# A routed two-choice network block: the residual written to the output early, and the experts' rows added to it in memory

## The chip, the cores and the metric

The kernel runs on one core of one Trainium2 chip. A core has five engines that run side by side: TensorE (PE in the profile; the loading of its weights is PEld), VectorE (DVE), ScalarE (ACT), GpSimd (POOL) and SyncE (SP), which here does nothing but issue transfers. The transfers themselves run on 16 DMA engines of the core, whoever issues them. The metric is the time of one execution on the device in microseconds (us).

## What is computed

Two layers work on `x`, 16 sequences of 128 tokens of 128 numbers. Each adds a block to the residual; only the end of the second matters here:

```python
x = x + _L0_ffn_ref(_L0_cond_ref(x, ...), ...)      # attention, then a dense network
x = x + _L1_ffn_ref(_L1_cond_ref(x, ...), ...)      # attention, then 8 experts, two choices per token
...
logits = x @ gate_w.T + gate_b                       # in _L1_ffn_ref, E, K = 8, 2; CAP = 320
probs = jax.nn.softmax(logits, axis=-1)
topk_prob, topk_idx = jax.lax.top_k(probs, K)
for c in range(K):
    buf_idx = jnp.where(pos < CAP, idx * CAP + pos, n_slots)
    xbuf = jnp.zeros((n_slots, Dm), x.dtype).at[buf_idx].set(x, mode='drop')
    hmid = jax.nn.relu(jnp.einsum('ecd,edf->ecf', xb, W1) + b1[:, None, :])
    yb = jnp.einsum('ecf,efd->ecd', hmid, W2) + b2[:, None, :]
    y = y + ytok * (prb * keep.astype(prb.dtype))[:, None]
```

So each of the 2048 tokens gets, on top of the residual, one row of 128 numbers from the expert of its first choice and one from that of its second.

## The kernel before

The residual stays in SBUF as `X` (128 tokens of each sequence on the partitions, 16 sequences, 128 numbers). The program goes through attention of the first layer (one batch per sequence), its dense network (four groups of four sequences), attention of the second layer (16 batches again, with the routing of earlier batches between them), and then the eight experts. Everything is float32. Each engine has its own written order; semaphores join them.

**Routing.** When a group of tokens is routed, POOL sends each row of `Y` (the normed token, its number and its weights) by an indirect DMA to the slot that its choice gives it, in one of two buffers in device memory, `slot_rows0` and `slot_rows1` (`scatter`, L637). Empty slots hold a row with a token number of 2048 and above.

**An expert** (`expert` on PE, DVE and ACT) works on 640 slots, 320 of each choice, in five tiles of 128 rows: SP loads them into `xb` (L482), PE turns them (L1122), multiplies by W1 (L1132), DVE and ACT add the bias and cut at zero (L1926, L1361), PE multiplies by W2 (L1142), DVE adds the second bias into `yb` (L1934), ACT scales by the token's weight (L1368). `yb` lies in `hT` for even experts and in `qn` for odd ones.

**The sends.** POOL sends the finished rows back, six indirect DMAs per expert, 48 in all, first and second choice in turn:

```python
SENDS = [(0, 0, P, 0), (2, DH, P, 1), (1, 0, P, 0), (3, 0, P, 1), (2, 0, DH, 0), (4, 0, P, 1)]   # tile, rows from, to, choice
```

The row's number says where it goes, in `choice_rows0` or `choice_rows1` (`back_d`), two buffers in device memory that were cleared in the first layer (`clear_back`, L468) and have 128 rows more than there are tokens, for the empty slots. Before a send, POOL waits until the tile is ready (`e_y`) and until the send before of the same choice has landed (`e_sent0`, `e_sent1`). DVE overwrites an expert's token numbers (`tags`, L1948) only when the sends of two experts before have landed.

**The end.** When all sends have landed, SP loads both buffers into `wide_buf` (L534, eight loads), DVE adds them to `X` (L1960, eight adds), SP stores `X` to the output (L538, four stores).

**SP in the second layer.** For each batch SP waits for the values `vp` and spreads them in six small transfers (L489, L492); behind them, in batches 2 to 7, it loads the weights of one expert (L474, L475).

Of the kernel before, what the change touches and what calls it, by code (L numbers as in the profile page):

```python
# [22 lines left out]
F32 = mybir.dt.float32  # L23
# [4 lines left out]
ALU = mybir.AluOpType  # L28
# [3 lines left out]
P = 128  # L32
NB = 16
# [4 lines left out]
EXPERTS = 8  # L38
CAP = 320
TOPK = 2  # L40
# [3 lines left out]
TOKENS = NB * P  # L44
BACK = TOKENS + P
# [15 lines left out]
LATE_DMAS = 6  # L61
REL_ROW = 6 * QB
REL_USED = 5 * QB
SCRATCH_ALL = 2 + 16 * (TOPK + TOPK * NB // 4)
FAR = -1e30
MASKED = -1e20
LN_EPS = 1e-5
# [2 lines left out]
def build(nc, a, out):  # L70
    ctx = ExitStack()
    with ctx:
        def sb(name, shape, dt=F32):
            return ctx.enter_context(nc.sbuf_tensor(name, shape, dt))
# [4 lines left out]
        def sem(name):  # L79
            return ctx.enter_context(nc.semaphore(name))  # L80

        def dram(name, shape, dt=F32):
            return nc.dram_tensor(name, shape, dt).ap()

        def at(ap, offset, dims):
            return bass.AP(ap.tensor, offset, dims)
# [1 line left out]

        rel_d = dram("rel_scratch", ((HEADS - 1) * QB * (REL_ROW - 1) + QB * REL_ROW,))
        slot_d = [dram(f"slot_rows{c}", (SLOTS + P, ROW)) for c in range(TOPK)]  # L90
        back_d = [dram(f"choice_rows{c}", (BACK, P)) for c in range(TOPK)]


        X = sb("X", [P, NB, P])
# [121 lines left out]
        wide_buf = sb("wide_buf", [P, TOPK * NB * P])  # L216
        empty = sb("empty", [P, ROW])
        zero_row = sb("zero_row", [P, 4, P])
# [12 lines left out]
              for v in (hT[:].rearrange("p i d -> p (i d)"), qn[:])]  # L231

        masked_bias = [wide_buf[:, i * BIAS_AT[-1]:(i + 1) * BIAS_AT[-1]] for i in range(2)]
        back = wide_buf[:].rearrange("p (c t d) -> p c t d", c=TOPK, t=NB)


        WoT = qsq[:].rearrange("p h d -> p (h d)")[:, 0:8 * P].rearrange("p (j d) -> p j d", j=8)
# [50 lines left out]
        s = {n: sem(n) for n in names}  # L288
# [12 lines left out]
        for n in ["ln_var", "ln_rstd", "g_T_psum", "g_rows", "g_WoT", "g_psum", "g_ready", "r_le", "r_exp",  # L301
                  "r_oh", "r_pos_read", "r_pos_psum", "r_pay", "slots_out0", "slots_out1",
                  "e_w", "e_x0", "e_x1",
                  "e_T_psum", "e_T", "e_h_psum", "e_h_act", "e_h_dve", "e_y_psum", "e_y_add", "e_y",
                  "back_in0", "back_in1", "back_in2", "back_in3", "z_step", "final_out",
                  "e_sent0", "e_sent1", "e_tags"]:
            s[n] = sem(n)

# [3 lines left out]
        def unit_bias(layer, u):  # L312
            return bias[layer][:, BIAS_AT[u]:BIAS_AT[u + 1]].rearrange(
                "p (h e k) -> p h e k", h=2, e=2)
# [13 lines left out]
        def over(eng, count, body, first=2, last=2):  # L328

            for t in range(first):  # L330
                body(t, t % 2)
            with eng.Fori(first // 2, (count - last) // 2) as k:
                body(2 * k, 0)
                body(2 * k + 1, 1)
            for t in range(count - last, count):
                body(t, t % 2)
# [20 lines left out]
        def no(t, value):  # L357
            return isinstance(t, int) and t == value
# [3 lines left out]
        def _(sp):  # L362
# [72 lines left out]
            for u in range(UNITS):  # L435
                v = unit_bias(0, u).rearrange("p h e k -> p (h e) k")
# [5 lines left out]
            def later_weights():  # L442
                spread(g_out[0][:], "L0_cond_g_out", P, late_in)
                sp.dma_start(Wq[1][:], a["L1_cond_Wq"]).then_inc(attw_in, 16)
                sp.dma_start(Wkv[1][:], a["L1_cond_Wkv"]).then_inc(attw_in, 16)
                sp.dma_start(Wo[1][:, :, 0:P], a["L1_cond_Wo"].rearrange("(j p) d -> p j d", p=P)).then_inc(attw_in, 16)
                for e in range(2):
                    sp.dma_start(Wkk[:, e, :], a["L1_cond_Wkv"][:, 0:DH]).then_inc(attw_in, 16)
                spread(fb2[:], "L0_ffn_b2", P, late_in)
                spread(g_out[1][:], "L1_cond_g_out", P, late_in)  # L450
                spread(gate_b[:], "L1_ffn_gate_b", EXPERTS, late_in)
                spread(mb2[:].rearrange("p e d -> p (e d)"), "L1_ffn_b2", EXPERTS * P, late_in)
                sp.dma_start(gate_rows[:], a["L1_ffn_gate_w"]).then_inc(late_in, 16)
# [11 lines left out]
                sp.dma_start(at(slot_d[c], 0, [[ROW, P], [P * ROW, SLOTS // P], [1, ROW]]),  # L465
                             empty[:].unsqueeze(1).broadcast_to([P, SLOTS // P, ROW])).then_inc(scratch_out, 16)

            def clear_back(c):  # L468
                for r in range(0, NB, 4):
                    sp.dma_start(at(back_d[c], r * P * P, [[P, P], [P * P, 4], [1, P]]),  # L470
                                 zero_row[:]).then_inc(scratch_out, 16)

            def load_expert(e):
                sp.dma_start(eW[e][:, 0, :], a["L1_ffn_W1"][e]).then_inc(s["e_w"], 16)  # L474
                sp.dma_start(eW[e][:, 1, :].rearrange("p (j d) -> p j d", j=FB),  # L475
                             a["L1_ffn_W2"][e].rearrange("(j p) d -> p j d", p=P)).then_inc(s["e_w"], 16)
# [7 lines left out]
            def spread_values(layer):  # L484
                def batch(b, i):
                    B = b + NB * layer
                    sp.wait_ge(s["v_ready"], B + 1)
                    for g in range(4):
                        sp.dma_start(vp_u0[i][QB * g:QB * (g + 1), g // 2, DH * (g % 2):DH * (g % 2 + 1)],  # L489
                                     vp[i][0:QB, :]).then_inc(s[f"vp_in{i}"], 16)  # L490
                    for e in range(2):
                        sp.dma_start(vp_u1[i][DH * e:DH * (e + 1), DH * e:DH * (e + 1)],  # L492
                                     vp[i][0:DH, :]).then_inc(s[f"vp_in{i}"], 16)
                    if layer == 0 and no(b, 0):
                        later_weights()
                    if layer == 0 and isinstance(b, int) and 1 <= b <= UNITS:
                        second_table(b - 1)
                    if layer == 0 and isinstance(b, int) and b in (5, 6):
                        clear_slots(b - 5)
                    if layer == 0 and isinstance(b, int) and b in (7, 8):  # L500
                        clear_back(b - 7)
                    if layer == 0 and isinstance(b, int) and b in (9, 10):
                        load_expert(b - 9)

                    if layer == 1 and no(b, 2):
                        sp.wait_ge(s["f_o_psum"], NB)
                    if layer == 1 and isinstance(b, int) and 2 <= b < EXPERTS:
                        load_expert(b)

                over(sp, NB, batch, EXPERTS if layer else 12)  # L510
# [15 lines left out]
                    sp.wait_ge(s["e_tags"], e + 1)  # L526
                    load_slots(e + 2, i)

            for c in range(TOPK):
                sp.wait_ge(s[f"e_sent{c}"], 16 * 3 * EXPERTS)  # L530
            for q in range(4):
                for c in range(TOPK):
                    src = at(back_d[c], 4 * q * P * P, [[P, P], [P * P, 4], [1, P]])
                    sp.dma_start(back[:, c, 4 * q:4 * q + 4, :], src).then_inc(s[f"back_in{q}"], 16)  # L534
            out_v = out.rearrange("b n d -> n b d")
            for q in range(4):
                sp.wait_ge(s["z_step"], 2 * (q + 1))
                sp.dma_start(out_v[:, 4 * q:4 * q + 4, :], X[:, 4 * q:4 * q + 4, :]).then_inc(  # L538
                    s["final_out"], 16)
            sp.wait_ge(s["final_out"], 64)  # L540


        @block.gpsimd
        def _(pool):
# [92 lines left out]
            def scatter(t, g):  # L637
                if t == GROUPS[0][0]:
                    pool.wait_ge(scratch_out, SCRATCH_ALL)
                if t == GROUPS[g][0]:  # L640
# [64 lines left out]
            for g in range(QUADS):  # L705
                v = X[:, 4 * g:4 * g + 4, :]
# [36 lines left out]
            def send(e, i):  # L743
                for n, (t, p0, p1, c) in enumerate(SENDS):
                    sent = 16 * 3 * e + 16 * (n // 2)
                    apart(pool, (s["e_y"], TILES * e + t + 1), (s[f"e_sent{c}"], sent))
                    pool.indirect_dma_start(back_d[c], bass.IndirectOffsetOnAxis(  # L747
                        tags[i][0:p1 - p0, t if p0 == 0 else TILES, 0:1].bitcast(U32), 0), yb[i][p0:p1, t, :],
                                            None).then_inc(s[f"e_sent{c}"], 16)

            over(pool, EXPERTS, send)


        @block.tensor
# [632 lines left out]
        def _(dve):  # L1387
# [565 lines left out]

            over(dve, EXPERTS, expert)
            result(EXPERTS - 1, 1, 1)
            for q in range(4):
                dve.wait_ge(s[f"back_in{q}"], 16 * TOPK)
                for c in range(TOPK):
                    v = X[:, 4 * q:4 * q + 4, :]
                    dve.tensor_tensor(v, v, back[:, c, 4 * q:4 * q + 4, :], ALU.add).then_inc(s["z_step"], 1)  # L1960
                    dve.wait_ge(s["z_step"], 2 * q + c + 1)


INPUTS = ["x", "cond_64", "fside_16xSxS_0", "mask_BxS_bf1", "mask_BxS_bk0", "L0_cond_g_norm", "L0_cond_Wq",
# [24 lines left out]
```

## Time and profile before

| | |
|---|---|
| time, median of 3 runs | 630.7 us (625.11 to 631.92) |
| the profiled execution | 627.16 us |
| its span in the profile | 625.4 us, so 1.8 us lie around the span |
| busy PE, DVE, ACT, POOL | 496.7, 433.3, 378.6, 309.3 us |
| mean granted TensorE clock | 0.933 of full speed |
| moved by DMA | 30.02 MB |

The span begins with the first instruction and ends with the last event. Busy times are sums of an engine's instructions; engines overlap. Times in rows are counted from the start of the span. An entry such as `[0.60 <-issue]` is the time that the engine stood idle before the instruction, and what ended it; "issue" means that the profile names nothing.

### The profile page before, as it was taken

To read this page: it belongs to the slowest core of one execution; us is meant where nothing else is said; L and a number is where in the kernel's file an instruction comes from. 1 tells how busy PE (TensorE), PEld (TensorE's weight loads), DVE (VectorE), ACT (ScalarE), POOL (GpSimd) and SP (SyncE) were. 2 spreads that over 40 slices of the span, in tenths; PEclk is the share of its full clock that TensorE was granted. 3 is DMA by queue.
4 is the path that set the end of the run, shared out by engine and by line. 5 is a ranking of instruction groups with operands and counts; after the bars stand their busy time and mean duration, and the time that the engine had idled before them with its cause. 6 is when DMAs were issued, how large, how long until landed. Compare 5 with 4: busy or idle time off the path is not lost.

```text
span 625.4 us, 13829 instructions
## 1 busy us (share of the span) xinstructions
PE 496.7 (79%) x3220; PEld 399.7 (64%) x3220; DVE 433.3 (69%) x2147; ACT 378.6 (61%) x1474; POOL 309.3 (49%) x366
## 2 busy tenths in 40 slices
PE   1366999999999978895799989988987707999940
PEld 0145777767777766564688878877875605887830
DVE  4496899999999986373668888889888631434323
ACT  1156788888888865671588878777866202444420
POOL 4282756656565641755433433533664460555560
PEclk9988899999999989996899999999999767999995
DMA  4640003723100000000011121000011112222117
GB/s 133 164 135 11 13 23 74 134 74 106 38 6 6 6 7 1 0 2 2 8 40 40 50 63 39 7 4 7 25 27 38 32 46 57 64 77 59 56 38 205
DMA packets 53302, 30.02 MB, mean 48 GB/s; under 512 B 19533, under 2 KB 49670, under 8 KB 53254
## 3 DMA queue, kind: packets, MB, share of 16 engines
q1 hardware_dynamic: 50694, 24.57, 15.6%
q0 software_dynamic: 2560, 4.90, 2.4%
q8 instruction: 18, 0.29, 0.2%
q14 instruction: 30, 0.25, 0.1%
HBM read 16.13 MB, written 11.22 MB: 44 GB/s over the span
## 4 chain that ended last, share of the span: by engine, by line
PE 46%; DVE 22%; issue 15%; SPq 4%; ACT 4%; POOL 3%; DMA 3%; DVEq 1%; ACTq 0%; POOLq 0%
PE psS L850 8%; DVE sc L1540 6%; PE psS L1142 5%; PE psQ L823 4%; PE psA L905 4%; PE psO L886 3%; PE psQ L1132 3%; PE psQ L807 3%; DVE centred L1601 2%; DVE OT L1561 2%; PE psT L868 2%; PE psO L1132 1%; PE psA L1132 1%; PE psQ L1066 1%; DVE qn L1531 1%
## 5 line engine op out<-in xcount | busy, mean ns | idle before, releaser
L1228 ACT ACTIVATE sc<-sc,negmax 128x97 f32<-128x97 f32 (+3 forms) x512 | 178.9, 353 | 36.8 <-DVE negmax L1540 35.5
L850 PE MATMUL psS<-kk,qT 128*128 128x194 f32 (+3 forms) x512 | 106.0, 330 | 29.1 <-DVE negmax L1540 27.2
L850 PEld LDWEIGHTS psS<-kk,qT 128*128 128x128 f32 x512 | 79.7, 195 | 56.0 <-issue 52.6
L1540 DVE CUSTOM_DVE_ANT_0 sc<-psS,wide_buf 128x97 f32<-128x97 f32 (+3 forms) x512 | 93.2, 237 | 29.9 <-PE psS L850 26.6
L632 POOL TENSOR_TENSOR wide_buf<-bias,mask 128x132 f32<-128x132 f32 (+3 forms) x128 | 108.8, 875 | 4.2 <-DVE negmax L1540 4.2
L1228 ACT ACTIVATION_READ_ACCUMULATOR sc<-sc,negmax 128x1 f32 x512 | 97.1, 190 | 0.0
L580 POOL TENSOR_TENSOR qrn<-qssc,half 128x9 f32<-128x9 f32 (+1 forms) x32 | 55.9, 1748 | 68.3 <-DVE qssc L1526 68.2
L1552 DVE TENSOR_TENSOR pn<-sc,rsum 128x128 f32<-128x128 f32 (+3 forms) x128 | 72.5, 566 | 8.0 <-DVE rsum L1548 0.2
L905 PE MATMUL psA<-Wo,OT 128*128 128x128 f32 (+1 forms) x512 | 66.0, 284 | 1.7 <-DVE OT L1561 1.7
L905 PEld LDWEIGHTS psA<-Wo,OT 128*128 128x128 f32 x512 | 63.0, 197 | 2.7 <-DVE OT L1561 2.5
L1561 DVE TENSOR_SCALAR OT<-psO,cols 128x512 f32<-128x512 f32 x64 | 47.6, 744 | 3.2 <-PE psO L886 1.8
L1241 ACT COPY PT<-psT 96x512 f32<-96x512 f32 x64 | 37.0, 577 | 14.5 <-PE psT L868 13.6
L868 PE MATMUL psT<-ident,pn 128*96 128x128 f32 (+1 forms) x256 | 40.2, 280 | 4.3 <-issue 2.2
L1540 DVE DVE_READ_ACCUMULATOR2_ANT negmax<- 128x1 f32 x512 | 41.3, 81 | 0.5 <-issue 0.5
L886 PE MATMUL psO<-PT,vp 96*64 96x256 f32 (+1 forms) x256 | 34.8, 390 | 7.3 <-DVE OT L1561 4.5
L644 POOL DMA_INDIRECT slot_rows<-Y,dest_u x32 | 31.3, 979 | 17.5 <-issue 7.2
L868 PEld LDWEIGHTS psT<-ident,pn 128*96 128x96 f32 (+1 forms) x256 | 28.6, 138 | 16.9 <-issue 16.3
L747 POOL DMA_INDIRECT choice_rows<-hT,tags x24 | 22.5, 939 | 32.7 <-ACT hT L1368 20.7
L807 PE MATMUL psQ<-Wq,xnT 128*128 128x512 f32 x64 | 36.6, 658 | 0.9 <-ACT qT L1210 0.2
L1210 ACT ACTIVATE qT<-psQ 128x512 f32<-128x512 f32 x64 | 34.6, 587 | 2.9 <-PE psQ L836 2.5
L615 POOL TENSOR_TENSOR vp<-kvs,vnull 128x64 f32<-128x64 f32 x32 | 11.7, 365 | 47.1 <-PE psO L886 47.0
L823 PE MATMUL psQ<-xnT,Wq 128*128 128x128 f32 x256 | 33.5, 287 | 0.0
(297 smaller groups left out, 1006.5 us busy)
## 6 DMA issues: line engine op xcount, KB each, us to landing
slot_rows<-empty SPq DMA_DIRECT2D x2, 1390.0 KB, 9.8
xb<-slot_rows SPq DMA_DIRECT2D x16, 139.0 KB
vp_u<-vp SPq DMA_DIRECT2D x128, 8.0 KB, 1.8
choice_rows<-zero_row SPq DMA_DIRECT2D x8, 256.0 KB, 3.0
wide_buf<-choice_rows SPq DMA_DIRECT2D x8, 256.0 KB, 4.7
Wq<-in_L_cond_Wq SPq DMA_DIRECT2D x2, 512.0 KB, 5.0
vp_u<-vp SPq DMA_DIRECT2D x64, 16.0 KB, 1.8
eW<-in_L_ffn_W SPq DMA_DIRECT2D x4, 256.0 KB, 2.9
```

Source lines behind the costliest of these rows:

```text
L580: pool.tensor_tensor(dst, src, half[:, 0:k], ALU.pow).then_inc(done, count)
L632: pool.tensor_tensor(unit_masked(i, u).rearrange("p h e k -> p (h e) k"), unit_bias(layer, u).rearrange("p h e k -> p (h e) k"), mask[laye ...
L807: pe.matmul(psQ[:, h, :], xnT[i][:], Wq[0][:, 512 * h:512 * (h + 1)], start=True, stop=True).then_inc(s["q_psum"], 1)
L823: m = pe.matmul(psQ[:, h, j * P:(j + 1) * P], Wq[1][:, (4 * h + j) * P:(4 * h + j + 1) * P], xnT[i][:], start=True, stop=True)
L850: m = pe.matmul(psS[:, h, 0:2 * w], qT[i][:, h, u].rearrange("p m q -> p (m q)"), kk[i][:, :, 0:w], start=True, stop=True)
L868: m = pe.transpose(psT[0:k, probs_bank(u, i), g * P:(g + 1) * P], pn[u][:, g, :], ident[:])
L886: m = pe.matmul(psO[DH * e:DH * (e + 1), 2 * P * (u - 2):2 * P * (u - 1)], vp[i][0:k, :], PT[u - 1][0:k, :, e, :], start=True, stop=True)
L905: m = pe.matmul(psA[:, Y_AT[layer]:4 * P], OT[i][:, j].rearrange("p u q -> p (u q)"), Wo[layer][:, j, :], start=(j == 0), stop=(j == 7))
L1228: m = act.activation(v, v, ACT.Exp, bias=negmax[:, u, g:g + 1], scale=-1.0, accum_out=psum_row[:, u, g:g + 1])
L1540: dve.tensor_tensor_reduce(sc[u][:, h, e, :], unit_psum(u)[:, h, e, :], unit_masked(i, u)[:, h, e, :], -1.0, -FAR, ALU.add, ALU.min, accum ...
L1552: dve.tensor_tensor(pn[u][:], sc[u][:].rearrange("p h e k -> p (h e) k")[:, :, 1:k + 1], rsum[:, u, :].unsqueeze(2).broadcast_to([P, 4, k] ...
L1561: dve.tensor_scalar(OT[i][:, :, 2 * half_of:2 * half_of + 2, :], psO[:].rearrange("p (u j q) -> p j u q", u=2, q=QB), cols[:, C_VN:C_VN + ...
```

## The change

- The residual is stored to the output by SP behind the spreads of batch 4 of the second layer (`store_residual`): four stores of 256 KB and one of zeros. The output has 128 rows more, which the caller drops; empty slots go there.
- First-choice sends go to the output itself and add to what is there (`compute_op=ALU.add`). Second-choice sends go, as before, plainly, to a cleared buffer, now `second_rows`. One clearing of the first layer falls away.
- POOL waits for the five stores before the first send. Behind the last send it waits for all sends and issues one transfer that adds the 2048 rows of `second_rows` to the output, from device memory to device memory, as 128 pieces of 8 KB.
- The eight loads, the eight adds of DVE and the four stores at the end fall away. SP ends by waiting for this last transfer.

```diff
-        back_d = [dram(f"choice_rows{c}", (BACK, P)) for c in range(TOPK)]
+        second_d = dram("second_rows", (BACK, P))
+        sums_d = out.rearrange("b n d -> (b n) d")
+        back_d = [sums_d, second_d]
...
+            def store_residual():
+                for q in range(4):
+                    sp.dma_start(out[4 * q:4 * q + 4].rearrange("b n d -> n b d"),
+                                 X[:, 4 * q:4 * q + 4, :]).then_inc(s["final_out"], 16)
+                sp.dma_start(sums_d[TOKENS:BACK, :], zero_row[:, 0, :]).then_inc(s["final_out"], 16)
...
-                    if layer == 0 and isinstance(b, int) and b in (7, 8):
-                        clear_back(b - 7)
+                    if layer == 0 and no(b, 7):
+                        clear_second()
+                    if layer == 1 and no(b, 4):
+                        sp.wait_ge(s["f_x"], NB)
+                        store_residual()
...
-            for c in range(TOPK):
-                sp.wait_ge(s[f"e_sent{c}"], 16 * 3 * EXPERTS)
-            for q in range(4):
-                for c in range(TOPK):
-                    src = at(back_d[c], 4 * q * P * P, [[P, P], [P * P, 4], [1, P]])
-                    sp.dma_start(back[:, c, 4 * q:4 * q + 4, :], src).then_inc(s[f"back_in{q}"], 16)
-            out_v = out.rearrange("b n d -> n b d")
-            for q in range(4):
-                sp.wait_ge(s["z_step"], 2 * (q + 1))
-                sp.dma_start(out_v[:, 4 * q:4 * q + 4, :], X[:, 4 * q:4 * q + 4, :]).then_inc(
-                    s["final_out"], 16)
-            sp.wait_ge(s["final_out"], 64)
+            sp.wait_ge(s["final_out"], 16 * 5)
+            sp.wait_ge(s["e_sent0"], 16 * 3 * EXPERTS)
+            sp.wait_ge(s["sums_out"], 16)
...
-                                            None).then_inc(s[f"e_sent{c}"], 16)
-
+                                            None, compute_op=ALU.add if c == 0 else ALU.bypass).then_inc(
+                                                s[f"e_sent{c}"], 16)
+
+            pool.wait_ge(s["final_out"], 16 * 5)
             over(pool, EXPERTS, send)
+            for c in range(TOPK):
+                pool.wait_ge(s[f"e_sent{c}"], 16 * 3 * EXPERTS)
+            pool.dma_start(sums_d[0:TOKENS, :].rearrange("(p r) d -> p (r d)", p=P),
+                           second_d[0:TOKENS, :].rearrange("(p r) d -> p (r d)", p=P),
+                           accum_op=ALU.add, max_dma_last_dim=8192).then_inc(s["sums_out"], 16)
...
-            for q in range(4):
-                dve.wait_ge(s[f"back_in{q}"], 16 * TOPK)
-                for c in range(TOPK):
-                    v = X[:, 4 * q:4 * q + 4, :]
-                    dve.tensor_tensor(v, v, back[:, c, 4 * q:4 * q + 4, :], ALU.add).then_inc(s["z_step"], 1)
-                    dve.wait_ge(s["z_step"], 2 * q + c + 1)
```

In the program of the changed kernel the lines below the new functions stand a few numbers higher. The end of SP's program, before:

```order
L482 DMA xb<-slot_rows 128x2x139
L520 REGISTER_ALU
L520 COMPARE_AND_BRANCH
L534 DMA wide_buf<-choice_rows 128x4x128 [waits e_sent1,e_sent0]
L534 DMA wide_buf<-choice_rows 128x4x128 x7
L538 DMA out_x<-X 128x4x128 [waits z_step] x4
L72 UNCONDITIONAL_BRANCH [waits final_out]
```

And with the change:

```order
L489 ISA
L489 DMA xb<-slot_rows 128x2x139
L530 REGISTER_ALU
L530 COMPARE_AND_BRANCH
L72 UNCONDITIONAL_BRANCH [waits sums_out,e_sent0,final_out]
```

Nothing is left on SP behind the loads of the slots but the waits. The end of POOL's program, where `qn` holds the last expert's rows, before:

```order
L747 DMA choice_rows<-qn,tags 2176x128 [waits e_sent1,e_y,const_done]
L747 DMA choice_rows<-qn,tags 2176x128 [waits e_sent0,e_y,const_done]
L747 DMA choice_rows<-qn,tags 2176x128 [waits e_sent1,e_y,const_done]
L72 UNCONDITIONAL_BRANCH
```

And with the change:

```order
L748 DMA second_rows<-qn,tags 2176x128 [waits e_sent1,e_y,const_done]
L748 DMA out_x<-qn,tags 2176x128 [waits e_sent0,e_y,const_done]
L748 DMA second_rows<-qn,tags 2176x128 [waits e_sent1,e_y,const_done]
L757 DMA out_x<-second_rows 128x2048 [waits e_sent1,e_sent0]
L72 UNCONDITIONAL_BRANCH
```

The sends stand where they stood, with other destinations; one transfer has come behind them. SP in batches 4 and 5 of the second layer, before:

```order
L492 DMA vp_u_0<-vp 64x64 x2
L474 DMA gT<-in_L_ffn_W 128x512
L475 DMA gT<-in_L_ffn_W 128x4x128
L489 DMA vp_u_1<-vp 32x64 [waits v_ready]
L489 DMA vp_u_1<-vp 32x64 x3
```

And with the change:

```order
L499 DMA vp_u_0<-vp 64x64 x2
L476 DMA out_x<-X 128x4x128 [waits f_x]
L476 DMA out_x<-X 128x4x128 x3
L478 DMA out_x<-zero_row 128x128
L481 DMA gT<-in_L_ffn_W 128x512
L482 DMA gT<-in_L_ffn_W 128x4x128
L496 DMA vp_u_1<-vp 32x64 [waits v_ready]
L496 DMA vp_u_1<-vp 32x64 x3
```

Five stores stand between the spreads of batch 4 and the weights of expert 4, and ahead of the spreads of batch 5.

## Rows read from the trace of the kernel before

**Rows 1.** The chain of waits, 595 to 625.4: start us, us, what.

```profile
600.54 0.99 ACT qn L1368 x3
...
603.24 0.75 POOL choice_rows L747
603.99 0.70 issue
604.69 0.74 POOL choice_rows L747
...
609.13 2.22 DMA choice_rows<-qn,tags
...
611.45 0.37 SPq L534
...
615.91 5.28 DMA wide_buf<-choice_rows
...
622.01 0.69 DVE X L1960
```

**Rows 2.** The timeline of POOL, 560 to 612: start us, us, engine, line.

```profile
563.00 0.96 POOL L747 DMA_INDIRECT choice_rows<-qn,tags  x1 [0.65 <-ACT qn L1368]
565.68 0.90 POOL L747 DMA_INDIRECT choice_rows<-qn,tags  x1 [1.72 <-DMA choice_rows<-qn,tags]
566.88 0.96 POOL L747 DMA_INDIRECT choice_rows<-qn,tags  x1 [0.30 <-issue]
...
601.68 0.96 POOL L747 DMA_INDIRECT choice_rows<-qn,tags  x1 [0.48 <-ACT qn L1368]
603.24 0.90 POOL L747 DMA_INDIRECT choice_rows<-qn,tags  x1 [0.60 <-issue]
604.69 0.96 POOL L747 DMA_INDIRECT choice_rows<-qn,tags  x1 [0.56 <-issue]
...
607.71 0.90 POOL L747 DMA_INDIRECT choice_rows<-qn,tags  x1 [0.61 <-issue]
```

**Rows 3.** The timeline, 518 to 560: sends of the first experts.

```profile
533.34 0.96 POOL L747 DMA_INDIRECT choice_rows<-hT,tags  x1 [19.47 <-ACT hT L1368]
...
543.02 0.96 POOL L747 DMA_INDIRECT choice_rows<-qn,tags  x1 [1.07 <-ACT qn L1368]
...
546.77 0.96 POOL L747 DMA_INDIRECT choice_rows<-qn,tags  x1 [0.30 <-issue]
...
549.78 0.90 POOL L747 DMA_INDIRECT choice_rows<-qn,tags  x1 [0.37 <-issue]
...
553.60 0.96 POOL L747 DMA_INDIRECT choice_rows<-hT,tags  x1 [0.30 <-issue]
```

**Rows 4.** Busy time in stretches: us, busy by engine, granted clock, DMA share, GB/s.

```profile
582.00:591.80 9.80, 9.65 (x64) 8.13 (x63) 3.71 (x11) 4.76 (x13) 5.22 (x7) 1.00 0.12 41
```

**Rows 5.** DMA queues, 533 to 611: packets, MB, share of 16 engines.

```profile
q0 software_dynamic: 1536, 2.62, 9.9%
```

**Rows 6.** DMA, 611 to 625.4: GB/s in 40 slices, packets, queue.

```profile
GB/s 0 0 0 0 68 124 321 319 346 320 242 195 240 280 256 299 314 323 314 327 300 282 290 299 304 322 341 340 299 189 302 300 147 9 0 243 290 195 0 0
DMA packets 6336, 3.15 MB, mean 219 GB/s; under 512 B 192, under 2 KB 6336, under 8 KB 6336
...
q1 hardware_dynamic: 6336, 3.15, 77.6%
```

**Rows 7.** DMA issues of the whole span: KB each, median us to landing.

```profile
vp_u<-vp SPq DMA_DIRECT2D x128, 8.0 KB, 1.8
...
bias<-in_fside_16xSxS SPq DMA_DIRECT2D x8, 8.0 KB, 1.8
```

**Rows 8.** The timeline of SP, 320 to 400: batches 4 and 5 of the second layer.

```profile
347.27 0.43 SPq L475 DMA_DIRECT2D gT<-in_L_ffn_W  x1
353.82 2.45 SPq L489 DMA_DIRECT2D vp_u<-vp  x4
```

**Rows 9.** The tile `out_x`: issues of its four stores, ns min/median/max.

```profile
L538 SPq DMA_DIRECT2D out_x<-X x4: 372/375/618, 616.7 to 622.7; - x4
```

**Rows 10.** The tile `choice_rows`: sends out of `qn`, ns min/median/max.

```profile
L747 POOL DMA_INDIRECT choice_rows<-qn,tags x24: 898/957/962, 543.0 to 609.1; - x24
```

More of the change, by code:

```diff
@@ L63 @@
 REL_USED = 5 * QB
-SCRATCH_ALL = 2 + 16 * (TOPK + TOPK * NB // 4)
+SCRATCH_ALL = 2 + 16 * (TOPK + NB // 4)
 FAR = -1e30
@@ L233, in build @@
         masked_bias = [wide_buf[:, i * BIAS_AT[-1]:(i + 1) * BIAS_AT[-1]] for i in range(2)]
-        back = wide_buf[:].rearrange("p (c t d) -> p c t d", c=TOPK, t=NB)
         WoT = qsq[:].rearrange("p h d -> p (h d)")[:, 0:8 * P].rearrange("p (j d) -> p j d", j=8)
@@ L304, in build @@
                   "e_T_psum", "e_T", "e_h_psum", "e_h_act", "e_h_dve", "e_y_psum", "e_y_add", "e_y",
-                  "back_in0", "back_in1", "back_in2", "back_in3", "z_step", "final_out",
+                  "sums_out", "final_out",
                   "e_sent0", "e_sent1", "e_tags"]:
@@ L466, in clear_slots, with clear_second @@
                              empty[:].unsqueeze(1).broadcast_to([P, SLOTS // P, ROW])).then_inc(scratch_out, 16)
-            def clear_back(c):
+            def clear_second():
                 for r in range(0, NB, 4):
-                    sp.dma_start(at(back_d[c], r * P * P, [[P, P], [P * P, 4], [1, P]]),
+                    sp.dma_start(at(second_d, r * P * P, [[P, P], [P * P, 4], [1, P]]),
                                  zero_row[:]).then_inc(scratch_out, 16)
+            def store_residual():
[3 more added lines that the diff above has]
+                sp.dma_start(sums_d[TOKENS:BACK, :], zero_row[:, 0, :]).then_inc(s["final_out"], 16)
             def load_expert(e):
@@ L1985 @@
         aps[name] = nc.dram_tensor("in_" + name, v.shape, mybir.dt.from_np(v.dtype), kind="ExternalInput").ap()
-    out = nc.dram_tensor("out_x", (NB, P, P), F32, kind="ExternalOutput").ap()
+    out = nc.dram_tensor("out_x", (NB + 1, P, P), F32, kind="ExternalOutput").ap()
     build(nc, aps, out)
-    return run_bass_kernel_spmd(nc, [arrays], core_ids=[0]).results[0]["out_x"]
+    return run_bass_kernel_spmd(nc, [arrays], core_ids=[0]).results[0]["out_x"][:NB]
```

## The prediction

> **What bounds the kernel now.** I read the chain of waits from its end first. ScalarE scales the last expert's first rows from 600.54 on. From there only POOL and transfers follow on the chain: POOL issues the last send at 609.13, the last send lands at 611.35, and then 14.05 us go by until 625.4 with SP's issues (611.45), the loads (5.28 us after the last issue), DVE's adds (0.69 each) and the stores [rows 1, 6]. So of the span's end some 24 us belong to the path that the change touches.
>
> The second thing to see is what paces POOL's sends. In the last expert all data are ready, yet the first-choice sends stand at 601.68, 604.69 and 607.71: steps of 3.01 and 3.02 us, with one second-choice send in each gap [rows 2]. The instruction itself takes 0.96 us [rows 10], and two that wait for nothing stand 1.2 us apart (565.68 and 566.88) [rows 2]. The chain tells why it is 3.01: the send of 604.69 was released at 603.99, which is 2.31 after the first-choice send of 601.68, and then took 0.70 to start [rows 1]. This is the wait of each send for the landing of the one before it of the same choice; 2.2 to 2.3 from issue to landing and 0.7 from landing to start. The last send shows the same, 2.22 [rows 1].
>
> The third is the pace of the expert. Between the first send of the first expert (533.34) and that of the last (601.68) lie 68.3 us, 9.76 each [rows 2, 3]. PE's stretch of one expert is 9.8 us with 9.65 of matmuls at full granted clock [rows 4]. Three steps of 3.01 make 9.03 on POOL. So PE bounds the experts and POOL has only 0.77 us per expert to spare, a quarter of a microsecond for each first-choice step. Some of that is spent: the second-choice send of 565.68 stood 1.72 for a late landing, and pushed the next first-choice send to 3.88 after the last (563.00 to 566.88) [rows 2].
>
> **What each part costs.** I sum against the profiled execution, 627.16 us, of which the span is 625.4; the median of the three runs shown is 630.7, 3.5 above it.
>
> The residual's stores. SP issues five more transfers in batch 4. The four at the end took 0.375 to issue, at most 0.62 [rows 9], so five cost 1.9 to 3.1. Queued behind them are the weights of expert 4, not needed for 200 us, and the spreads of batch 5. SP's last issue in that batch ends at 347.7 and the next begins at 353.82 [rows 8], 6.1 us of idle cover. The 1.1 MB at the 340 GB/s of the best slices [rows 6] take 3.3 us and the weights behind them 1.6, so the rings are empty about when the spreads come. I take 0; if the cover were gone, the spreads of one batch would be up to 3 us late, once. POOL's new wait for these stores has all 48 sends queued behind it, but it is passed some 180 us before POOL gets there. SP's wait for the last residual update is met in batch 0. The clearing that falls away in the first layer had no one waiting: 0.
>
> The adding sends, the disputed term. Now an engine must read the destination as well as the source before it writes. No row of this trace shows such a transfer, so I bound what it adds to the 2.31 from issue to landing. From below: 0, if both reads go side by side; a read from device memory is not slower to land than one from SBUF (8 KB from `fside` 1.8, 8 KB from `vp` 1.8) [rows 7]. One pass of the data over an engine is small: 9.9% of 16 engines over 78 us is 123.6 us, over 48 sends and 16 engines 0.16 us [rows 5]. A second read as one more pass adds 0.16. If each of an engine's eight rows goes as a piece by itself, twice, at the 28 ns of the 512-byte packets at the end (77.6% of 16 x 14.4 us over 6336 packets) [rows 6], it is 16 x 28 = 0.45 in place of 0.16, which adds 0.29. Longer lists to write add a little: a 64-row send (603.24) took 0.90 and a 128-row one (604.69) 0.96 [rows 2], so 0.06 for twice the entries. From above: 1.8, a whole further round trip, if the read must land before the write sets out [rows 7]. I take 0.35 (0.29 + 0.06), the row nearest to the same pieces of 512 bytes, and 0 to 1.8 as the bounds.
>
> The Trainium skill, "Collectives: The Full Stack", Part 3 (the bandwidth ceiling), says that an adding transfer is slower because it reads two sources and not because of the add, and so runs at half the copy's rate. No row here shows it. By it alone the term would be the one more pass, and the sends would end some 2 us earlier than I sum.
>
> With 0.35 the first-choice step becomes 3.01 + 0.35 = 3.36, and three of them 10.08, more than PE's 9.8: POOL becomes the bound of the experts. The last expert's first send is the 22nd of its choice, 21 steps behind the first: 533.34 + 21 x 3.36 = 603.9. Late landings like the one at 565.68 may come on top; three first-choice steps show such a loss: 543.02 to 546.77, 549.78 to 553.60 and the 3.88 above, which are 0.74, 0.81 and 0.87 over 3.01, 2.4 in all [rows 2, 3]. I keep half of it. That gives 605.1 for 601.68, 3.4 later, and the two steps that follow add 0.7. The sends end 4.1 us later, at 615.4. PE, DVE and ACT are then held back by POOL, which costs nothing more: an expert's tags wait for the sends of two experts before, and from there to its first ready tile lie some 3 us, against 10 that POOL is busy with the expert between.
>
> The end. Before, 14.05 us from the last landing. Now POOL starts 0.70 after the landing, and the transfer needs the 2.22 of a small one plus its bytes. A plain pass of 1.05 MB at 330 GB/s (the slices of the loads show 321 to 346 [rows 6]) is 3.2; the add reads two sources, so 6.4. Sum 0.7 + 2.2 + 6.4 = 9.3, and 4.7 saved. Bounds: 6.1 for one pass (7.9 saved) and, at 3.15 MB over all passes and the stretch's mean of 219 GB/s, 14.4 + 2.9 = 17.3 (3.3 lost). The adds of DVE and the twelve transfers of SP are inside the 14.05 and need no term of their own.
>
> Sum: 627.16 + 4.1 - 4.7 = 626.6, a change of -0.6. On the median that is 630.
>
> **The rivals.** First, **the add is free**: the reads go side by side, the step stays 3.01, and the last transfer runs at the plain rate. Then nothing is lost and 7.9 saved: 630.7 - 7.9 = 622.8. For it speak the equal 1.8 of the two kinds of read; against it that twice the bytes must be read by the same engines. The Trainium skill's page "DMA: Bandwidth & Descriptors" (Anatomy of one DMA, SWDGE path) gives such a transfer 2.0 us plus its bytes at 436 GB/s, which is 4.4 for 1.05 MB; by it the end would take 5.1 and the time be near 622. The 2.22 of the last send agrees with its fixed part.
>
> Second, **the first-choice chain**, the case on the other side. The new step is multiplied by 23, since each adding send waits for the landing of the one before. At 1.0 us more per send, the last expert begins at 533.34 + 21 x 4.01 = 617.6, 15.9 later, and ends 17.9 later with its two steps; less 4.7 that is +13.2, 644. At the bound of 1.8 it is +31.6, 662. It decides from 0.39 on (nothing gained), and from 0.65 on the loss passes 6.3 us. For it: POOL has 0.25 us per step to spare and the chain repeats; nothing shown says that reading, adding and writing eight rows overlap.
>
> Third, **the last transfer is slow**: 17.3 us in place of 9.3 with the sends as I forecast them gives +7.4, 638. Between device memory and device memory every byte crosses there three times; against it, the pieces are of 8 KB and not 512 bytes.
>
> Fourth, **the change doesn't save what it says**, because the stores in batch 4 or late clearing delay attention: up to +3, which would be hidden within the first case.
>
> **How the numbers follow.** Three runs spread over 1.1%, so about 1% (6.3 us) is what a measurement of this kernel can tell from no change. Forecast (added latency 0.1 to 0.65, end near 9): 0.47, 625 to 637. Free add: 0.15, 622.8, just over the 1%. Chain: 0.28, 637 to 662. Slow last transfer: 0.07, 638. Others: 0.03, counted as slower. So faster 0.15, same 0.47, slower 0.38. The likeliest is 630; the range 623 to 650 leaves out the upper half of the chain's case and a little below.
>
> **What would show it.** In the changed kernel: the distance between first-choice sends to `out_x` with data ready (3.4 forecast; 3.0 for the free add; 4 or more for the chain); PE's stretch per expert, 9.8 if POOL keeps up, near 10.1 or longer if it doesn't; the last landing at 615; from it to the end 9.3; the spreads of batch 5 at their old distance behind those of batch 4. I am wrong if the added latency is outside 0.1 to 0.65, if second-choice sends get slower too, or if PE's granted clock falls while it waits for POOL: its stretch of an expert shows 1.00 now, and half of that would make PE the bound again, at nearly 19 us per expert.

## The result: 2.4% slower

| | before | changed |
|---|---|---|
| median, 4 runs each | 629.48 us (625.11 to 631.92) | 646.64 us (642.26 to 647.0) |
| ratio | | 1.0243, 95% interval 1.0209 to 1.0277 |
| profiled execution, span | 627.16, 625.4 us | 646.5, 644.7 us |
| first send of the experts | 533.34 | 536.41 |
| last landing of a send | 611.35 | 632.65 |
| from there to the end | 14.05 us | 12.05 us |

The ratio and its interval are the numbers to go by, here and below; the quotient of two medians differs a little from it (1.027 here). The span grew by 19.3 us: 3.1 before the first send, 18.2 between the first send and the last landing (78.0 before, 96.24 now), and -2.0 at the end. I don't count the first part to the change. In the eleven kernels of the experiments, which are alike up to there but for stores and clearing, the first send stood anywhere from 530.9 to 539.2, and in the one that adds only the change's stores to the kernel before, at 533.36.

The chain of waits of the changed kernel, 600 to 645 (start us, us, what), answers to [rows 1]:

```profile
616.71 3.08 DMA out_x<-hT,tags
...
620.57 3.23 DMA out_x<-qn,tags
623.80 0.02 issue
...
623.87 0.72 issue
624.59 3.26 DMA out_x<-qn,tags
...
630.40 2.25 DMA second_rows<-qn,tags
...
633.23 1.00 POOLq L72
```

No computation is left on it. It goes from one adding send to the next (the whole view has one plain send between them, at 610.52): 3.02 to 3.30 from issue to landing, and about 0.8 until the next starts. The plain send at 630.40 lands in 2.25, as plain sends did [rows 1]. The timeline of POOL in the same stretch, against [rows 2]:

```profile
620.57 1.57 POOL L748 DMA_INDIRECT out_x<-qn,tags  x1 [1.11 <-DMA out_x<-hT,tags]
622.44 0.92 POOL L748 DMA_INDIRECT second_rows<-qn,tags  x1 [0.30 <-issue]
624.59 1.57 POOL L748 DMA_INDIRECT out_x<-qn,tags  x1 [1.23 <-DMA out_x<-qn,tags]
626.47 0.98 POOL L748 DMA_INDIRECT second_rows<-qn,tags  x1 [0.30 <-issue]
628.63 1.46 POOL L748 DMA_INDIRECT out_x<-qn,tags  x1 [1.18 <-DMA out_x<-qn,tags]
630.40 0.98 POOL L748 DMA_INDIRECT second_rows<-qn,tags  x1 [0.30 <-issue]
633.26 0.98 POOL L757 DMA_DIRECT2D out_x<-second_rows  x1 [1.88 <-DMA second_rows<-qn,tags]
```

The steps are 4.02 and 4.04 where they were 3.01 and 3.02. From the first send (536.41) to the 22nd of the first choice (620.57) lie 84.2 us, a mean of 4.01 over 21 steps, of which the single ones run from 3.66 to 4.53. In the kernel before the same 21 steps took 68.3 us, 3.25 each. The instruction takes 1.57 and not 0.96, and for a send of 64 rows (628.63) 1.46 and not 0.90. The second-choice send waits for nothing but the one ahead of it on POOL (0.30 of idle, in all of the 24 but the one at 595.42); the first-choice send waits 1.1 to 1.2 for a landing.

The queue of POOL's transfers, 533 to 633 (packets, MB, share of 16 engines), against [rows 5]:

```profile
q0 software_dynamic: 3712, 2.62, 18.4%
```

The bytes are the same 2.62 MB, the packets 3712 in place of 1536: every added row is a packet of its own (2560 rows and 1152 others). They take 18.4% of 16 x 100 us, 294 us, against 124 before.

A narrow window of the same view shows the packets of one send of 128 rows alone. First a plain one of the kernel before, issued at 604.69 (window 605.99 to 606.99, a slice is 0.025 us), then an adding one of the changed kernel, issued at 624.59 (window 626.49 to 627.89, a slice is 0.035 us):

```profile
GB/s 0 0 0 0 0 0 0 0 0 328 655 328 328 492 328 0 165 0 0 0 0 0 0 0 0 0 0 0 0 0 0 0 0 0 0 0 0 0 0 0
q0 software_dynamic: 32, 0.07, 16.6%
```

```profile
GB/s 0 0 0 0 0 0 15 88 29 59 29 73 59 88 117 132 146 117 146 190 88 161 132 73 44 44 29 15 0 0 0 0 0 0 0 0 0 0 0 0
q0 software_dynamic: 144, 0.07, 51.5%
```

The plain send's packets begin 1.52 us after its issue and last 0.2; the adding send's begin 2.11 after it and last 0.77. They keep each engine busy for 0.17 and 0.72 us (16.6% of 1.0 and 51.5% of 1.4 us). So the longer instruction does delay the landing: its 0.61 goes with the 0.59 by which the first packet comes later.

The end. Each engine's program closes with an instruction that the profile names DRAIN; the profile shows the last marks of all engines only when all of these are over. The instructions of the closing line, before and then changed (engine, operation, ns min/median/max, start):

```profile
L72 POOLq DRAIN  x1: 7797/7797/7797, 608.9 to 608.9; - x1
...
L72 SPq COMPARE_BRANCH  x1: 38/38/38, 625.0 to 625.0; - x1
```

```profile
L72 POOLq DRAIN  x1: 11250/11250/11250, 633.2 to 633.2; - x1
L72 SPq COMPARE_BRANCH  x1: 38/38/38, 641.2 to 641.2; - x1
```

SP sees the last transfer landed at 641.2, 7.9 us after its issue. POOL's drain goes on until 633.2 + 11.25 = 644.5, and the span ends at 644.7. Before, the drain behind the last send ended at 616.7, under SP's loads, and cost nothing.

The residual's stores, SP's timeline, against [rows 8]:

```profile
346.29 2.52 SPq L476 DMA_DIRECT2D out_x<-X  x4
348.86 0.85 SPq L478 DMA_DIRECT2D out_x<-zero_row  x1
...
353.58 2.45 SPq L496 DMA_DIRECT2D vp_u<-vp  x4
```

They took 3.4 us of the idle 6, and the spreads of batch 5 come where they came.

### The profile page after: what moved, and what is told of

The parts are those of the page before. It is cut to its first block, busy times and chain, and to the rows that moved or that the text cites. A ratio compares the mean times of both kernels' runs of the same rounds, so it can differ in the third digit from the quotient of the medians.

```text
span 644.7 us, 13808 instructions
## 1 busy us (share of the span) xinstructions
PE 498.2 (77%) x3220; PEld 400.6 (62%) x3220; DVE 429.2 (67%) x2139; ACT 378.3 (59%) x1474; POOL 325.8 (51%) x367
## 4 chain that ended last, share of the span: by engine, by line
PE 41%; DVE 22%; issue 17%; DMA 7%; ACT 3%; SPq 3%; POOL 3%; DVEq 1%; POOLq 0%; ACTq 0%
PE psS L858 7%; DVE sc L1548 6%; PE psQ L831 4%; PE psA L913 4%; PE psS L1150 3%; PE psO L894 3%; DMA out_x<-qn,tags 3%; PE psQ L815 2%; DVE centred L1609 2%; PE psQ L1140 2%; DVE OT L1569 2%; PE psT L876 2%; DMA out_x<-hT,tags 1%; DVE qn L1539 1%; DVE qss L1528 1%
## 5 line engine op out<-in xcount | busy, mean ns | idle before, releaser
L858 PEld LDWEIGHTS psS<-kk,qT 128*128 128x128 f32 x512 | 79.4, 194 | 55.3 <-issue 52.2
L1560 DVE TENSOR_TENSOR pn<-sc,rsum 128x128 f32<-128x128 f32 (+3 forms) x128 | 74.6, 583 | 8.0 <-DVE rsum L1556 0.2
L913 PE MATMUL psA<-Wo,OT 128*128 128x128 f32 (+1 forms) x512 | 67.9, 289 | 1.1 <-DVE OT L1569 1.1
L913 PEld LDWEIGHTS psA<-Wo,OT 128*128 128x128 f32 x512 | 64.9, 201 | 2.0 <-DVE OT L1569 1.9
L748 POOL DMA_INDIRECT out_x<-hT,tags x12 | 18.5, 1543 | 32.5 <-ACT hT L1376 19.5
```

Source lines behind the costliest of these rows:

```text
L858: m = pe.matmul(psS[:, h, 0:2 * w], qT[i][:, h, u].rearrange("p m q -> p (m q)"), kk[i][:, :, 0:w], start=True, stop=True)
L913: m = pe.matmul(psA[:, Y_AT[layer]:4 * P], OT[i][:, j].rearrange("p u q -> p (u q)"), Wo[layer][:, j, :], start=(j == 0), stop=(j == 7))
L1560: dve.tensor_tensor(pn[u][:], sc[u][:].rearrange("p h e k -> p (h e) k")[:, :, 1:k + 1], rsum[:, u, :].unsqueeze(2).broadcast_to([P, 4, k] ...
```

## The experiments

The theory after the result: an adding send lands about 1 us later than a plain one, and since each waits for the landing of the one before, that is paid once per first-choice send. Rivals: it is the destination and not the adding; POOL's longer instruction or the DMA engines' time is what adds up. Times of each group are against the kernel before in runs of the same chip.

**First-choice sends that do not add.**

```diff
-  None, compute_op=ALU.add if c == 0 else ALU.bypass)
+  None, compute_op=ALU.bypass)
```

> The changed kernel with its first-choice sends not adding: they overwrite the residual in the output, which is so left out of the result. Everything else stays. Theory 1 (the adding itself makes the send late to land, and the chain of first-choice sends repeats it): steps between first-choice sends go back from 4.0 to 3.0 us, the instruction from 1.57 to 0.96, and the time to about 628. Theory 2 (it is the destination, the output, or the stores before): the steps stay near 4.0 and the time near 646.

627.15 us against 628.27, ratio 0.9962 (0.9927 to 0.9997). The timeline of POOL:

```profile
604.75 0.96 POOL L748 DMA_INDIRECT out_x<-qn,tags  x1 [0.60 <-ACT qn L1376]
...
607.75 0.96 POOL L748 DMA_INDIRECT out_x<-qn,tags  x1 [0.66 <-issue]
...
610.76 0.90 POOL L748 DMA_INDIRECT out_x<-qn,tags  x1 [0.71 <-issue]
```

Steps of 3.00 and 3.01, the instruction at 0.96. The destination and the stores before are out; the adding is all of the loss. What remains of the change (the new end) is 0.4% faster by the ratio, which is at the edge of the noise; in the traces it is the 2.0 us between the last landing and the end.

**Every other first-choice send adds**, the chain left as it is.

```diff
-  compute_op=ALU.add if c == 0 else ALU.bypass
+  compute_op=ALU.add if c == 0 and (i + n // 2) % 2 == 0 else ALU.bypass
```

> The changed kernel with every other first-choice send adding and the others overwriting, all in one chain; the rows overwritten lose their residual. If each adding send makes its step 1.0 longer and nothing else matters, steps alternate between 4.0 and 3.0, an expert takes POOL 10.5 us against 9.8 of PE, and the sends take 6 to 8 us longer than plain ones: about 634. If it is not the single send's landing but something that adds up over time, the steps do not follow the kind of the send before them.

637.46 us against 628.58, ratio 1.0150 (1.0106 to 1.0195), 3.5 above what I wrote.

```profile
611.92 0.96 POOL L748 DMA_INDIRECT out_x<-qn,tags  x1 [1.19 <-DMA out_x<-hT,tags]
...
614.92 1.61 POOL L748 DMA_INDIRECT out_x<-qn,tags  x1 [0.83 <-DMA out_x<-qn,tags]
...
618.92 0.90 POOL L748 DMA_INDIRECT out_x<-qn,tags  x1 [1.11 <-DMA out_x<-qn,tags]
```

The step behind the plain send is 3.00, behind the adding one 4.00. So the cost goes with the single send. The steps of 3.0 and 4.0 hold where all data are ready; over the first 21 steps the mean is 3.68 and not 3.5, with late ones up to 4.66, which is 3.7 us in all.

**Second-choice sends add too** (their buffer's rows for empty slots are cleared as well).

```diff
-  compute_op=ALU.add if c == 0 else ALU.bypass
+  compute_op=ALU.add
```

> The changed kernel with its second-choice sends adding too (to the cleared buffer; same result). Theory 1a (each chain waits for its own landing, and the two run side by side): issues of 1.57 + 0.3 + 1.57 + 0.3 = 3.7 fit into the present step of 4.0, so the step becomes 4.0 to 4.2 and the time stays within 4 us of the changed kernel. Theory 1b (POOL's time per send, or the DMA engines, set the pace): each step grows by 0.6 or more, 23 times, and the time by 14 or more, to 660.

649.32 us against 628.27, ratio 1.0316 (1.0244 to 1.0387), which lies over the changed kernel's 1.0243 by 0.7% with overlapping intervals, so the times alone do not show a difference. In the traces it is 101.6 us from the first send to the last landing against 96.2: twenty-four more adding sends cost 5.4 us, where the first 24 cost 18. That is a little over the 4 us that I had allowed and far from 14. From the first send (532.67) to the 22nd of the first choice (621.15) the mean step is 4.21; the last ones are 4.02 and 3.94. Two adding sends issued back to back still fit into one landing and restart; what adds up is not how long POOL and the engines are busy in all, but the chain, in which each landing counts (and in it the longer instruction of that one send).

**Two chains for the first choice.** Every other adding send goes to another cleared buffer with its own semaphore.

```diff
+  third_d = dram("third_rows", (BACK, P))
+  first_d = [sums_d, third_d]
...
+  k = (i + m) % 2
+  name, dst = ("e_sent0", "e_sent2")[k], first_d[k]
```

> The changed kernel with every other first-choice send adding to a second cleared buffer with its own semaphore, so that an adding send waits for the landing of the one two before it. These rows are left out of the result. Theory 1a (the wait for the landing): the step falls from 4.0 to what POOL issues, 1.57 + 0.3 + 0.98 + 0.3 = 3.15, which is under PE's 9.8 per expert; the sends end about 17 us earlier and the time is 628 to 632. Theory 1b (the pace is set by POOL or the engines): step 4.0, 646.

627.12 us against 628.27, ratio 0.9978 (0.9943 to 1.0013).

```profile
602.36 1.57 POOL L767 DMA_INDIRECT third_rows<-qn,tags  x1 [0.30 <-issue]
...
605.45 1.57 POOL L767 DMA_INDIRECT out_x<-qn,tags  x1 [0.30 <-issue]
...
608.62 1.46 POOL L767 DMA_INDIRECT third_rows<-qn,tags  x1 [0.30 <-issue]
```

The adding sends are as long as ever, and the steps are 3.09 and 3.17: what POOL issues. This settles it: with the same adds and without the wait for the last landing, the loss is gone.

**Half the bytes.** The adding sends carry 64 of 128 numbers.

```diff
+  half_d = dram("half_rows", (BACK, P // 2))
...
+  yb[i][p0:p1, t, 0:P if c else P // 2]
```

> The changed kernel with its first-choice sends adding only 64 of the 128 numbers of each row, to a cleared buffer of such rows, which is left out of the result. Same number of rows, half the bytes. If the bytes make the adding send late, the step falls from 4.0 by half of the 0.9 that adding costs, to 3.6; if it is a cost per row and per send, the step stays within 0.15 of 4.0 and the instruction at 1.57.

One run, 642.92 us; two steps at the end:

```profile
617.39 1.57 POOL L757 DMA_INDIRECT half_rows<-qn,tags  x1 [1.03 <-DMA half_rows<-hT,tags]
...
621.17 1.57 POOL L757 DMA_INDIRECT half_rows<-qn,tags  x1 [0.99 <-DMA half_rows<-qn,tags]
...
625.07 1.46 POOL L757 DMA_INDIRECT half_rows<-qn,tags  x1 [1.04 <-DMA half_rows<-qn,tags]
```

Steps of 3.78 and 3.90, 0.24 and 0.14 under 4.02 and 4.04; between the two answers that I had written. Half the bytes save about a fifth of what adding costs, and the instruction stays at 1.57. So most of the cost does not go with the bytes; this run does not part what is paid per send from what is paid per row.

**The last transfer as a plain copy, from POOL and from SP.** Both results hold the second-choice rows alone.

```diff
-                           accum_op=ALU.add, max_dma_last_dim=8192).then_inc(s["sums_out"], 16)
+                           max_dma_last_dim=8192).then_inc(s["sums_out"], 16)
```

> The changed kernel with its last transfer copying and not adding, so the result is the second-choice rows alone. If reading two sources costs what I forecast, the transfer lands in about 4.7 instead of 7.9 us and the time falls by 3; if the add there is free, nothing changes. The 3.4 us between the last landing and the end (POOL's drain) stays in both.

641.97 us against 628.27, ratio 1.0212 (1.0134 to 1.0289). The transfer is issued at 628.04 and SP sees it at 633.6, 5.6 us in place of 7.9.

```diff
-            pool.dma_start(sums_d[0:TOKENS, :].rearrange("(p r) d -> p (r d)", p=P),
...
+            sp.dma_start(sums_d[0:TOKENS, :].rearrange("(p r) d -> p (r d)", p=P),
+                         second_d[0:TOKENS, :].rearrange("(p r) d -> p (r d)", p=P)).then_inc(s["sums_out"], 16)
```

> The changed kernel with the last transfer issued by SP as a plain copy, so the second-choice rows alone are the result. It stands against the run in which POOL issued the same plain copy and in which 3.4 us lay between its landing and the end. Theory: those 3.4 us are POOL's drain, which starts to count with the last transfer that POOL issued; here that is the last send, so the drain runs beside SP's copy and the time falls by 3 us or a little more against that run, to 638. Rival: any transfer between two places in device memory keeps the end waiting: then 642.

639.29 us against 630.48, ratio 1.0151 (1.0110 to 1.0193). The closing lines, POOL's copy first, then SP's:

```profile
L72 POOLq DRAIN  x1: 8893/8893/8893, 628.0 to 628.0; - x1
L72 SPq COMPARE_BRANCH  x1: 38/38/38, 633.6 to 633.6; - x1
```

```profile
L72 POOLq DRAIN  x1: 8646/8646/8646, 628.2 to 628.2; - x1
L72 SPq COMPARE_BRANCH  x1: 38/38/38, 637.3 to 637.3; - x1
```

Issued by POOL, the copy is followed by 3.3 us in which only the drain runs (to 636.9). Issued by SP at 631.54, it lands at 637.3, the drain is over at 636.8, and 0.3 us later the span ends. From the issue of the copy to the end of the span it is 9.1 us from POOL (628.04 to 637.1) and 6.1 from SP. The drain follows POOL's own last transfer and not SP's copy: it ends 3.3 us behind the landing of a direct transfer and, where POOL's last one is an indirect send, 5.3 to 5.4 behind that (636.8 here, where SP, which waits for that landing, issued at 631.54; 611.35 and 616.7 in the kernel before). The two intervals overlap, so the gain in time itself (0.6% between the ratios) is not shown by the ratios alone; the closing lines show it.

**The stores alone.** The kernel before, with its own end, and the five stores with a semaphore of their own.

```diff
+  if layer == 1 and no(b, 4):
+      sp.wait_ge(s["f_x"], NB)
+      store_residual()
```

> The kernel before with the residual's five stores in batch 4 of the second layer added, and its own end kept. I forecast 0 for them: within 2 us of the kernel before. If they delay attention or the weights, the first send of the experts stands later than 531 to 536 us and the time grows by 3.

630.35 us against 630.48, ratio 0.9994 (0.9966 to 1.0021), first send at 533.36. They cost nothing.

**A version that waits less.** The experiments point to a kernel that keeps the change whole and loses the chain. Each choice has two semaphores in turn, and the empty slots of neighbouring sends go to different rows.

```diff
+  BACK = TOKENS + 2 * P
...
+  name = f"e_sent{c}{(i + m) % 2}"
+  sent = 24 * e + 16 * (m // 2) if i == 0 else 24 * (e - 1) + (16, 32, 32)[m]
```

> The changed kernel, full computation, with two semaphores for each choice in turn, so that a send waits for the one two before it of its choice; the rows of empty slots go to 256 rows in place of 128, so that no two sends in flight write the same row. By theory 1a the steps fall to POOL's issue of 3.15, PE bounds the experts again, the last landing is at about 612 for a first send at 533, and the end of 12 us is kept: 625 to 628, at or 1 to 3 us under the kernel before. If two adding sends in flight slow each other, it stays above 632.

629.2 us against 630.48, ratio 0.998 (0.9955 to 1.0005), full computation.

```profile
605.17 1.57 POOL L753 DMA_INDIRECT out_x<-qn,tags  x1 [0.68 <-ACT qn L1382]
607.05 0.92 POOL L753 DMA_INDIRECT second_rows<-qn,tags  x1 [0.30 <-issue]
608.27 1.58 POOL L753 DMA_INDIRECT out_x<-qn,tags  x1 [0.30 <-issue]
```

The step is 3.10, the last expert's first send waits for its data again, and the whole loss of the change is made good: 2.6% under the changed kernel by the two ratios. Against the kernel before it is not to be told apart. From the last landing (615.44) to the end (627.6) it takes 12.2 us, 1.9 less than before, and from the first send (536.04) to that landing 79.4, 1.4 more than the 78.0 of before.

**The same without the change**: the kernel before with two semaphores for each choice, and a control with the 256 rows alone (the first of these lines without the second).

```diff
+  BACK = TOKENS + 2 * P
...
+  name = f"e_sent{c}{(i + m) % 2}"
```

> The kernel before, full computation, with two semaphores for each choice in turn and 256 rows for empty slots, no adding transfer. PE bounds the experts already, so only the last expert's six sends gain: from one in 1.5 us to one in 1.26, 1 to 1.5 us in all, 0.2% under the kernel before. If a wait for the landing costs also elsewhere, more.

> The kernel before, full computation, with 256 rows for empty slots and its one semaphore per choice kept. In the run with two semaphores per choice each expert's first result was taken by DVE 2.3 us late and the experts took 10.5 us each. If the rows for empty slots or the longer clearing did that, it shows here too and the time is at or over 631; if it comes with the second semaphores or the closer sends, the experts take 9.8 us and the time is that of the kernel before within 1 us.

632.11 us against 628.58, ratio 1.0057 (1.0029 to 1.0085): a miss, slower where I expected 0.2% faster. The sends did come every 1.26 us in the last expert, but each expert took 10.5 us and not 9.8. DVE took an expert's first result only when the second was near:

```profile
571.63 0.56 DVE L1939 TENSOR_TENSOR hT<-psS,mb 128x384 f32<-128x384 f32 x1 [4.56 <-remote]
...
582.16 0.56 DVE L1939 TENSOR_TENSOR qn<-psS,mb 128x384 f32<-128x384 f32 x1 [4.70 <-remote]
```

In the kernel before this idle time is 2.2 to 3.3 ("remote" is the profile's word for a release that it puts to none of the engines here). The control gave 630.13 against 629.41, ratio 1.0014 (0.9994 to 1.0034), with 68.4 us from the first expert's result to the eighth's, 9.8 each, so the rows for empty slots are not the cause. What in the closer sends or the second semaphores holds DVE's result back stays open; the kernel above, which has the second semaphores too, does not show it (its experts took 9.9).

## Why the prediction was wrong

Read against its own steps:

- **What bounds.** Right. The loss came in through the first-choice chain at 3.01 and the 0.77 us to spare per expert. That the landing of the send before sets the 3.01 is shown too: with two semaphores for each choice the kernel before sends every 1.26 us in its last expert.
- **The stores.** Right at 0. SP needed 3.4 us for them, just over the 3.1 of the upper bound, under a cover of 6.
- **The adding send, the step that failed.** I took 0.35 more per send, 0.29 of it for data and 0.06 for the longer instruction; the step grew by 1.00. The landing came 0.9 later (3.23 to 3.26 against 2.31) and the restart 0.1. The instruction was the error that counted. I scaled it by the difference between 64 and 128 rows, which gave 0.06; it grew by 0.61, the first packet came 0.59 later, and as the 64-row send grew by 0.56 too, over 0.5 of that is a charge per adding instruction (an estimate from these two). No row of the kernel before showed one. The 1.0 was inside my bounds of 0 to 1.8 and beyond the 0.65 at which I had put the loss at 1%.
- **Its data part.** It was of the right kind, rows going one by one, but its 0.45 us per engine was put together wrongly: it is not 16 pieces of 28 ns but nine packets (144 over 16 engines) of 80 ns, 0.72 for 128 rows and 0.60 as the mean of the 24 sends (294 us of packets, less the 62 of the 24 plain sends at the rate of [rows 5]). The packets last 0.57 longer than a plain send's, but only 0.38 lies between the last one and the landing where it was 0.58, so the data part took some 0.35 of the landing and my 0.29 was near it by luck. Why such a packet takes 80 ns, and why the part behind the last packet is shorter, stays open.
- **The multiplication.** Right: a mean of 4.01 over 21 steps makes 12.0 us per expert on POOL, over PE's 9.8, and with 1.0 the prediction's second rival ends the sends 17.9 later against 18.2 measured. That it comes so close is in part luck: most steps behind sends of 64 rows are shorter (3.66 to 3.86), late ones longer (up to 4.53), and the two happen to cancel. PE waited for POOL as described (DVE idle 19.9 us on the tags for sends of two experts before), at full granted clock, and made no bubble in POOL's chain:

```profile
591.80:601.70 9.90, 7.22 (x49) 6.00 (x48) 2.60 (x9) 2.60 (x9) 5.90 (x5) 1.00 0.18 28
```

- **The end.** 9.3 forecast, 12.05 measured. The part that I costed took 0.6 to the issue and 7.9 to the landing, 8.5 together; the plain copy of the experiment 5.6, so the adding, with its second read, costs 2.3 where I had 3.2. The rest is POOL's drain, 3.3 us beyond the landing, and 0.2 behind it, which I did not look for. It was in the trace of before, hidden under the loads. With it 2.0 is saved and not 4.7.
- **The choice.** The likeliest was -0.6 us, the rival of the chain had a chance of 0.28 and 644 at 1.0 us; the measured 646.64 lies in its case and in the range of 623 to 650. The free add is refuted by the step of 4.0 and by the last transfer: 7.9 us, and 5.6 as a plain copy. The Trainium skill, "DMA: Bandwidth & Descriptors" (Anatomy of one DMA, SWDGE path), gives 2.0 us plus the bytes at 436 GB/s, by which I had estimated 4.4; the trace does not agree, not even for the plain copy. The Trainium skill, "Collectives: The Full Stack" (Part 3, the bandwidth ceiling), says that an adding transfer is slower because of its second read and not because of the add. No run separates the read from the add here. In the last transfer the adding one takes 5.7 us beyond the 2.2 of a small send and the plain copy 3.4, a factor of 1.7. In the small sends a second read of the kind that I took for one more pass (0.16 by [rows 5]) does not cover it, for each engine is busy 0.72 in place of 0.17.
- **Two sums.** With the 0.16 of one more pass the step is 3.17 and three of them 9.51, under PE's 9.8, so the sends would end 0.3 later than before, 3.8 earlier than I summed and not some 2. And with the late landings in it, as in my forecast, the sum breaks even at 0.375 and not at 0.39. Neither changes a chance or the range.

## What to carry to other kernels

Where each transfer waits for the landing of the last, any latency added to one is paid once for each; count the links before you count the bytes, and compare the new step with what hides it (here a quarter of a microsecond). In this kernel adding sends came at no loss once two such chains ran in turn; I kept two sends in flight from writing the same row, and no run shows what happens if they do. Where POOL issues the last transfer, count its drain too (3.3 us here behind the landing). A plain copy issued by SP did not pay it; no run has SP issue an adding transfer.

## What the runs showed of the hardware

- An adding indirect send of 128 rows of 512 bytes to device memory: instruction 1.57 us against 0.96, first packet 2.11 us after the issue against 1.52, landing 3.2 to 3.3 against 2.2 to 2.3; for 64 rows the instruction takes 1.46 against 0.90. With half the bytes per row the step is 0.14 to 0.24 shorter.
- It goes out as one packet per row; a plain one of the same rows does not (144 packets against 32 for one send of 128 rows; 3712 against 1536 for 48 sends of which 24 add). The packets keep each engine busy for 0.72 us against 0.17.
- 1.05 MB from device memory to device memory in pieces of 8 KB: 7.9 us adding, 5.6 us plain from POOL, 5.8 us plain from SP (631.54 to 637.3).
- POOL's drain at the end of the program lasts until 3.3 us after the landing of its last direct transfer, and until 5.4 us after that of its last indirect send (611.35 to 616.7).
